# Value products of two key tiles in one run, with three quads of weights kept, in a second attention layer

## What is computed

```python
qh, kh, vh = (proj(q, Wq, bq), proj(k, Wk, bk), proj(v, Wv, bv))
scores = jnp.einsum('bhqd,bhkd->bhqk', qh, kh) / math.sqrt(D)
scores = jnp.where(mask[:, :, :, None] == 0, jnp.float32(-1000000000.0), scores)
attn = jax.nn.softmax(scores, axis=-1)
out = jnp.einsum('bhqk,bhkd->bhqd', attn, vh)
concat = out.transpose(0, 2, 1, 3).reshape(b, -1, E)
return concat @ Wo.T + bo
```

## Time and profile before

| what | value |
|---|---|
| median of 3 runs | 2132.16 us |
| lowest and highest of them | 2129.74 and 2134.51 us |
| span of the profiled execution, first to last instruction | 2142.8 us |
| TensorE busy in it | 1832.9 us (86%) |
| VectorE busy | 1060.1 us (49%) |
| ScalarE busy | 907.4 us (42%) |
| exponentials of both layers (line 736) | 1024, 500.6 us busy |
| reductions of both layers (line 868) | 896, 522.6 us busy |
| value products of both layers (line 708) | 2048 instructions, 233.8 us busy |

### The profile page before, as it was taken

The page is one execution under the profiler, slowest core; times in us unless marked ns, Lnnn a source line. Parts: engine busy times, 40 slices in busy tenths (PEclk is TensorE's granted clock), DMA queues, the critical chain, the costliest instruction groups (busy, mean ns, idle before and its releaser), DMA issues. The chain is left out here.

```text
span 2142.8 us, 30068 instructions
## 1 busy us (share of the span) xinstructions
PE 1832.9 (86%) x10491; PEld 1040.9 (49%) x10491; DVE 1060.1 (49%) x2734; ACT 907.4 (42%) x1876; POOL 598.0 (28%) x577
## 2 busy tenths in 40 slices
PE   2789999999864999636899999998972999999995
PEld 1445555555543777413334444443331566666664
DVE  3456777787744444234867777777420212211211
ACT  1456666665641222113577777775650111111110
POOL 1312111220002787503111232221123233333322
PEclk9999999999976999858999999999985999999998
DMA  2544454434223777524323433331114133333314
GB/s 86 158 120 146 147 173 142 129 123 133 74 72 102 165 174 169 91 72 150 107 71 115 133 97 94 115 115 52 42 41 139 31 79 79 75 74 79 74 25 98
DMA packets 204245, 222.86 MB, mean 104 GB/s; under 512 B 33438, under 2 KB 195231, under 8 KB 203431
## 3 DMA queue, kind: packets, MB, share of 16 engines
q1 hardware_dynamic: 176458, 177.48, 27.2%
q0 software_dynamic: 27648, 43.60, 10.7%
HBM read 155.06 MB, written 86.93 MB: 113 GB/s over the span
## 5 line engine op out<-in xcount | busy, mean ns | idle before, releaser
L868 DVE TENSOR_REDUCE nmx<-mxb 128x1 f32<-128x512 f32 (+1 forms) x896 | 522.6, 608 | 299.7 <-PE mxb L681 155.1
L736 ACT ACTIVATE pt<-stb 128x512 f32<-128x512 f32 (+3 forms) x1024 | 500.6, 519 | 284.3 <-PE stb L697 144.1
L681 PE MATMUL mxb<-kst,qst 96*128 96x512 bf16 (+4 forms) x1024 | 332.7, 347 | 34.0 <-DVE nmx L868 22.9
L694 PE MATMUL stb<-qst,kst 99*128 99x512 bf16 (+4 forms) x1024 | 342.8, 345 | 15.1 <-DMA qst<-m3T 8.2
L708 PE MATMUL ob<-pt,va 128*32 128x512 f32 (+3 forms) x2048 | 233.8, 528 | 3.8 <-ACT oT L741 2.6
L1421 PE MATMUL e_h_bank<-e_xT,e_w 128*128 128x512 f32 x512 | 226.0, 600 | 6.1 <-ACT e_xT L1461 5.4
L1435 PE MATMUL e_y_bank<-e_w,e_h 128*128 128x256 f32 x1024 | 226.9, 379 | 0.0
L694 PEld LDWEIGHTS stb<-qst,kst 102*128 102x128 bf16 (+1 forms) x1024 | 99.8, 98 | 257.1 <-ACT pt L736 161.1
L1435 PEld LDWEIGHTS e_y_bank<-e_w,e_h 128*128 128x128 f32 x1024 | 192.9, 190 | 31.8 <-issue 7.2
L1118 POOL TENSOR_TENSOR qk<-qk,parts 128x512 f32<-128x512 f32 x64 | 72.8, 1158 | 437.0 <-ACT qk L769 226.4
L1575 POOL DMA_INDIRECT x_after_l<-e_y,e_token x64 | 99.5, 1555 | 282.0 <-DVE e_y L1540 267.3
(11 more groups left out here) (226 smaller groups left out, 2503.4 us busy)
## 6 DMA issues: line engine op xcount, KB each, us to landing
qk_parts<-parts SPq DMA_DIRECT2D x16, 1536.0 KB, 6.0
qst<-qk_parts SPq DMA_DIRECT2D x384, 64.0 KB, 2.2
kst<-qk_parts SPq DMA_DIRECT2D x384, 64.0 KB, 2.2
e_w<-in_L_ffn_w SPq DMA_DIRECT2D x16, 1024.0 KB
rows<-rows SPq DMA_DIRECT2D x15, 1060.0 KB, 8.9
crow<-in_ctx SPq DMA_DIRECT2D x16, 512.0 KB
x_after_l<-xres SPq DMA_DIRECT2D x16, 512.0 KB, 3.2
e_gu_nat<-in_L_ffn_gate_up_proj SPq DMA_DIRECT2D x64, 128.0 KB
```

The lines of the kernel that those rows point to most:

```text
L681: last = pe.matmul(out, qst[par][0:rows_used, h, qt * P:(qt + 1) * P], kst[par][0:rows_used, h, 0:nk], start=True, stop=not causal)
L694: last = pe.matmul(out[:, q0:S], kst[par][0:ROWS, h, kt * P:(kt + 1) * P], qst[par][0:ROWS, h, q0:S], start=True, stop=not causal)
L736: act.activation(pt[:, u % 8, q_from(kt):S], stb[(STEPS * b + u) % N_ST][:, q_from(kt):S], ACT.Exp, scale=SCALE).then_inc(s["st_free"], 1)
L868: last = dve.tensor_reduce(nmx[:, qt, h:h + 1], got[:, at:at + k_to(qt)], AX.X, ALU.max, negate=True)
```

## The change

In the second layer the value products of key tiles 0 and 1 are made in one run of sixteen instructions at u = 10 of the group's sixteen steps, and those of tiles 2 and 3 in one run two steps into the next group (u = 18 counted from the group's start). The runs of the four steps between fall away, so a batch has eight runs. `pt` has twelve slots, three quads in turn, and ScalarE's wait ahead of a quad is for the run that holds the quad three before. The waits of the runs count accordingly: the first run of a group waits for the exponentials of two key tiles, and for the free output bank at u = 10 where it was u = 6. The counts of the semaphore `pt_free` are per run, so the copy of the output bank and of the values wait for two counts a group in place of four. The first layer's tables give the runs, slots and waits that it had. A packed form of the score banks is written but switched off (`PACKED = False`).

```diff
+    PACKED = False
+    SCORE_BANKS = score_banks(PACKED)
+    N_SCORE = len(SCORE_BANKS)
+    SCORE_NO = {u: i for i, u in enumerate(sorted(SCORE_BANKS))}
+    VALUE_CALLS = {6: (0,), 10: (1,), 14: (2,), 18: (3,)} if causal else {10: (0, 1), 18: (2, 3)}
+    N_CALL = len(VALUE_CALLS) * GROUPS
+    USED = {at: {kt for up_to in VALUE_CALLS if up_to <= at for kt in VALUE_CALLS[up_to]} for at in VALUE_CALLS}
+    PT_SLOTS = 8 if causal else 12
...
-        pt = t_("pt", [P, 8, S])
+        pt = t_("pt", [P, PT_SLOTS, S])
...
+        def quad(b, u):
+            return (STEPS * b + u) // 4
+
+        def slot(b, u):
+            if PACKED:
+                return SCORE_NO[u] % (N_SCORE // GROUPS)
+            return quad(b, u) % (PT_SLOTS // 4) * 4 + u % 4
...
-            def values(b, g, kt):
-                if g == 0 and kt == 0:
+            def values(b, g, call):
+                at = sorted(VALUE_CALLS)[call]
+                if g == 0 and call == 0:
                     pe.wait_ge(evac["v"], 2 * b + 2)
-                pe.wait_ge(s["st_free"], STEPS * b + 16 * g + 4 * kt + 4)
-                if kt == 0:
+                scored = sum(u < 16 * (g + 1) and u // 16 == g and {kt for _, kt, _ in SCORE_BANKS[u]} <= USED[at] for u in SCORE_BANKS)
+                pe.wait_ge(s["st_free"], N_SCORE * b + N_SCORE // GROUPS * g + scored)
+                if call == 0:
                     wait(pe, s["ob_evac"], 4 * b + g)
-                q0 = q_from(kt)
-                for j in range(4):
-                    last = pe.matmul(ob[32 * j:32 * j + 32, q0:S], va[b % 3][:, kt, 4 * g + j, :],
-                                     pt[:, 4 * (kt % 2) + j, q0:S], start=kt == 0, stop=kt == NT - 1,
-                                     tile_position=(0, 32 * j))
+                for kt in VALUE_CALLS[at]:
+                    for j in range(4):
+                        last = pe.matmul(ob[32 * j:32 * j + 32, q_from(kt):S], va[b % 3][:, kt, 4 * g + j, :],
+                                         weights_of(b, g, kt, j), start=kt == 0, stop=kt == VALUE_CALLS[max(VALUE_CALLS)][-1],
+                                         tile_position=(0, 32 * j))
                 last.then_inc(s["pt_free"], 1)
...
-                    if u == 2 and prev is not None:
-                        values(prev, 3, 3)
-                    if u % 4 == 2 and u > 2 and cur is not None:
-                        values(cur, (u - 6) // 16, (u - 6) % 16 // 4)
+                    for call, at in enumerate(sorted(VALUE_CALLS)):
+                        if u == at - 16 and prev is not None:
+                            values(prev, GROUPS - 1, call)
+                        if u >= at and (u - at) % 16 == 0 and cur is not None:
+                            values(cur, (u - at) // 16, call)
...
-                if u % 4 == 0:
-                    wait(act, s["pt_free"], 16 * b + u // 4 - 1)
+                if not PACKED and u % 4 == 0:
+                    last = quad(b, u) - PT_SLOTS // 4
+                    wait(act, s["pt_free"], last // (4 // len(VALUE_CALLS)) + 1)
...
-                act.wait_ge(s["pt_free"], 16 * b + 4 * g + 4)
+                act.wait_ge(s["pt_free"], N_CALL * b + len(VALUE_CALLS) * (g + 1))
```

More of the change, by code:

```diff
@@ L246, in shared_banks, with score_banks @@
     return banks
+def score_banks(packed):
+    banks = {}
+    for g in range(GROUPS):
+        if not packed:
+            banks.update({16 * g + u: ((4 * g + u % 4, u // 4, 0),) for u in range(16)})
+            continue
+        for j, u in enumerate((0, 2, 3, 5)):
+            banks[16 * g + u] = ((4 * g + j, 0, 0),)
+        for j, u in enumerate((7, 8, 10, 11)):
+            banks[16 * g + u] = ((4 * g + j, 3, 0), (4 * g + j, 1, P))
+        for j, u in enumerate((13, 15)):
+            banks[16 * g + u] = ((4 * g + 2 * j, 2, 0), (4 * g + 2 * j + 1, 2, 2 * P))
+    return banks
 def attention(c, layer, x_in, ctx_in, mask, wq, bq, wk, bk, wv, bv, wp, bp, wroute, x_out, rows,
@@ L491, in k_to, with weights_of @@
             return (qt + 1) * P if causal else S
+        def quad(b, u):
[4 more added lines that the diff above has]
+            return quad(b, u) % (PT_SLOTS // 4) * 4 + u % 4
+        def weights_of(b, g, kt, j):
+            if not PACKED:
+                return pt[:, slot(b, 16 * g + 4 * kt + j), q_from(kt):S]
+            at, first = {0: (0, j), 1: (P, 4 + j), 2: (2 * P * (j % 2), 8 + j // 2), 3: (0, 4 + j)}[kt]
+            return pt[:, first, at:at + S - q_from(kt)]
         @block.sync
@@ L518, in stack @@
                 sp.wait_ge(s["parts_out"], 16 * (n + 1))
-                wait(sp, s["st_full"], STEPS * (n - 2) + 16 * g + 16)
+                wait(sp, s["st_full"], N_SCORE * (n - 2) + N_SCORE // GROUPS * (g + 1))
                 for side, dst, terms in ((0, qst, Q_TERM), (1, kst, K_TERM)):
@@ L687, in scores @@
             def scores(b, u):
-                par, g, kt, j = b % 2, u // 16, u % 16 // 4, u % 4
+                par = b % 2
                 if u % 32 == 0:
                     pe.wait_ge(s[f"shift_in{u // 32}"], 48 * (b + 1))
[L691 to L695, removed]
@@ L696, in scores @@
-                if causal:
-                    last = pe.matmul(out[:, q0:q0 + P], c.identb[:, :], c.hide_st[:, :], start=False, stop=True)
+                if u not in SCORE_BANKS:
+                    return
+                no = N_SCORE * b + SCORE_NO[u]
+                wait(pe, s["st_free"], no - N_ST + 1)
+                bank = stb[no % N_ST]
+                for h, kt, at in SCORE_BANKS[u]:
+                    to = at if PACKED else q_from(kt)
+                    last = pe.matmul(bank[:, to:to + S - q_from(kt)], kst[par][0:ROWS, h, kt * P:(kt + 1) * P],
+                                     qst[par][0:ROWS, h, q_from(kt):S], start=True, stop=not causal)
+                    if causal:
+                        last = pe.matmul(bank[:, to:to + P], c.identb[:, :], c.hide_st[:, :], start=False, stop=True)
@@ L731, in exps @@
             def exps(b, u):
-                kt = u % 16 // 4
-                if u % 4 == 0:
-                    wait(act, s["pt_free"], 16 * b + u // 4 - 1)
-                act.wait_ge(s["st_full"], STEPS * b + u + 1)
-                act.activation(pt[:, u % 8, q_from(kt):S], stb[(STEPS * b + u) % N_ST][:, q_from(kt):S], ACT.Exp, scale=SCALE).then_inc(s["st_free"], 1)
+                if u not in SCORE_BANKS:
+                    return
+                no = N_SCORE * b + SCORE_NO[u]
+                if PACKED and u % 16 in (0, 7):
+                    wait(act, s["pt_free"], N_CALL * b + u // 16 * 2 - (1 if u % 16 == 0 else 0))
+                if not PACKED and u % 4 == 0:
+                    last = quad(b, u) - PT_SLOTS // 4
+                    wait(act, s["pt_free"], last // (4 // len(VALUE_CALLS)) + 1)
+                act.wait_ge(s["st_full"], no + 1)
+                q0 = 0 if PACKED else q_from(SCORE_BANKS[u][0][1])
+                act.activation(pt[:, slot(b, u), q0:S], stb[no % N_ST][:, q0:S], ACT.Exp, scale=SCALE).then_inc(s["st_free"], 1)
             def outputs(b, g):
-                act.wait_ge(s["pt_free"], 16 * b + 4 * g + 4)
+                act.wait_ge(s["pt_free"], N_CALL * b + len(VALUE_CALLS) * (g + 1))
                 wait(act, full["o"], 4 * b + g - 1)
@@ L759, in evacuate @@
                     if t == 0 and b > 2:
-                        act.wait_ge(s["pt_free"], 16 * (b - 2))
+                        act.wait_ge(s["pt_free"], N_CALL * (b - 2))
                     act.activation(va[b % 3][:, 2 * t:2 * t + 2, :, 0:DH],
```

## The result

The changed kernel takes 2168.57 us (median of 4 runs, 2159.42 to 2172.81) against 2130.95 us for the kernel before on the same chips: a ratio of 1.0169 with a 95% interval of 1.0147 to 1.0191, slower. I had forecast 2152 us in a range of 2125 to 2167: the sign was right, the size was half of what came, and the median lies 1.6 us above the range.

A forecast was written before the change was run, and what follows sets the result against it. TensorE's order was taken as the bound; 2.6 us slower in each of seven iterations (18.1), +1 for the last and +0.9 for its final run made +20 us on the 2132.16 median: 2152 us, range 2125 to 2167.

The forecast's parts named there:

- What bounds it: Second attention layer: TensorE's order is the bound, busy 70.67 of 71.37 us, and one periodic iteration can be followed on paper.
- A run of two tiles: Merged value run holds TensorE 2.00 us (bounds 2.00 and 2.18) against 2.18 for two runs, saving 0.18 a pair.
- Projection late by 0.57, statistics by 0.59, reductions by 0.83: Stretches u = 10 to 18, 18 to 26 and 26 to 34, each longer by the respective us in an iteration.
- The other five stretches: Rest of an iteration: about +0.6 us together, bounds -0.9 and +2; four lose 0.1 to 0.3, u = 42 to 50 gains.
- Seven iterations at the full price, +1 for the last, +0.9 for its run: Second layer's eight iterations: seven at 2.6 us give 18.1; last iteration +1 (-1.5 to +4), very last run +0.9.
- Waits on the reductions: Sign of being right: TensorE's waits for the maxima's reductions over the layer become several times 14.5 us.
- Runs at u = 26 and 34 later, at u = 50 not: Sign of being right, within an iteration: those two value runs start later, the one at u = 50 does not.
- TensorE as the plain bound: Rival, 12%: TensorE stays the bound and 11.8 us come off: 2120 us, an iteration near 69.9 us.
- The tiles do merge: Answers a rival, 8%: the two key tiles don't merge, a pair still costs 2.18 us: 2164 us.
- Nothing cancelled: Answers a rival, 7%: late chains half as long eat the 11.8 us gain: 2132 us, within 4 us.

The follow-up runs named there:

- e10_two_moved: The changed kernel with two groups of output transposes and their normalisations moved, u = 39 to 42 and 55 to 57: 2159.30 us, ratio 1.0145 to before.
- e5_after_half: The changed kernel with the second layer's maxima reductions reading half a bank: 2131.21 us, ratio 1.0004 to before.
- e8_placed: The changed kernel with merged runs one step later and the second layer's other work moved, some work banks swapped: 2123.43 us, ratio 0.9962 to before.
- e9_placed_separate: The moved work of e8_placed, but with separate runs of one tile at u = 7, 11, 15, 19: 2139.42 us, ratio 1.0037 to before.

## Why the prediction was right in sign and half the size

- *What bounds it*: right. TensorE's order sets an iteration, and one iteration read on paper gave the stretches 10 to 34 to within 0.1 us each.
- *A run of two tiles*: 2.00 us predicted, 1.95 measured, 0.05 outside the lower bound, which supposed that no pass takes less than 0.45. Two more passes took 1.95 - 1.09 = 0.86. The Trainium skill, page TensorEngine Tiling (Array Packing), section Tiling Modes, says that a change of tiling mode, and not just of tile, drains TensorE. The trace agrees in so far as sixteen products of one mode (1181.90, all 128 by 32) hold TensorE for 0.23 us less than two runs of eight; how much of that is a drain no run here shows.
- *Projection late by 0.57, statistics by 0.59, reductions by 0.83*: 0.67, 0.52 and 0.86. Right.
- *"The other five stretches, by the same accounts over their own steps, come to about +0.6 together"*: **the step that failed**. They came to +2.22, beyond the estimate's upper bound of +2. I had worked through three stretches and guessed the rest as late exponentials and reductions. What I did not follow was the two work banks: who used the bank last, and what stood between. The three waits for `m3T` and `base` are 1.53 us; e10_two_moved took 1.07 away. The rows did not show it, since a bank that is free in time has no row; the table `TRIPS` could, with its bank in the last column. The Trainium skill, page Perfetto Trace Analysis, section Optimizing Tensor Performance (Matmuls), has independent groups of products rotate through banks so that one's emptying lies beside the next's products. The trace agrees, with 0.29, 0.49 and 0.75 us where a bank came round too soon.
- *Seven iterations at the full price, +1 for the last, +0.9 for its run*: five pay the full price; the first pays 0.5, the seventh 5.7, the last 3.3. In the last ones the granted clock is a second price that I had none of: about 4 us for the sixth iteration where it falls. From the forecast of 2152 us the median is 16.6 us away. The price of the five stretches, 1.6 us in each of five iterations, is some 8 of these; another 9 lie between the profiled execution of after (2159.42 us at a mean granted clock of 0.939) and the median, half of whose executions had 0.932 or 0.933.
- *Waits on the reductions "several times 14.5 us"*: wrong. Over the layer they are 16.5 us in a window with the start that the 14.5 had, tens of microseconds ahead of the layer's first score product; from that product on they are 6.7 us before and 11.4 after. The waits view of the kernel after, same window start:

```profile
PE mxb L718 <- DVE nmx L918: 16.5, 46, 1.0
...
PE stb L735 <- ACT pt L786: 5.3, 16, 1.1
PE work L659 <- ACT m3T L858: 5.2, 12, 0.8
PE work L659 <- DVE base L1026: 5.0, 6, 1.0
...
PE work L670 <- ACT onT L804: 4.6, 7, 0.8
```

  The waits for `m3T`, `base` and `onT`, 14.8 us here, are the larger part of what is new, and e5_after_half shows that most of the loss stays when VectorE is relieved.
- *Runs at u = 26 and 34 later, at u = 50 not*: right; 42 to 50 is 0.24 shorter, which is the merging's 0.23 and nobody late.
- *The rivals*: TensorE as the plain bound would have given 69.5 us an iteration; it needs e8_placed's placing to come near, 70.25. The tiles do merge. Nothing cancelled.

Left open: what decides whether the clock falls in a given execution, and why e9_placed_separate loses 1.4 us to before; neither was tried.

## What to carry to other kernels

In an order that is written out by hand, a short piece of work on the bounding engine is also the time in which others empty banks for it; before you bunch such pieces, list for every step behind a vacated place which bank it writes, who empties it, and what stood between. Average slack of the other engines (18 us an iteration here) says nothing about this. A saving of 0.23 us a pair was real in every kernel with merged runs and twelve slots, but it was only kept where the steps around it were placed again.

## What was not expected of the hardware

Two more passes of a packed f32 run cost 0.43 us each where the first is followed at 0.45, so a run of sixteen is cheaper than its rows of eight suggested. And in executions of one program, ten microseconds with the same TensorE work (7.67 us busy) are followed at a granted clock of 1.00 in one and 0.85 in the other, with 8.68 and 9.88 us for the stretch u = 26 to 34.
